# State-space stage: the second half's step size made by GpSimd inside the rounds, one convolution and the direct term on TensorE

## The reference, cut to what matters

```
x = einsum(in_proj_w, ctx)                       # per half: 256 channels x 512 positions
xc = depthwise causal conv(x, conv_w), 4 taps
u = silu(xc + conv_b)
dt_lo, Bm, Cm = split(x_proj_w @ u)              # 8, 16 and 16 rows
delta = softplus(dt_proj_w @ dt_lo + dt_proj_b)  # the step size
A = -exp(A_log)
for t: state = state * exp(delta_t * A) + (delta_t * u_t) * B_t ;  y_t = state . C_t
y = y + D * u
y = y * silu(z)                                  # z is the layer-normed x
```

## Time and profile before

| | us |
|---|---|
| median of 3 runs | 1015.46 (1014.79 to 1017.61) |
| the profiled execution, whole | 1015.46 |
| its span in the trace | 1012.7 |
| TensorE busy in the span | 911.6 (90%) |
| VectorE busy | 718.1 (71%) |
| ScalarE busy | 646.1 (64%) |
| GpSimd busy | 484.5 (48%) |

### The profile page before, as it was taken

One profiled execution on the slowest core, in us unless ns is written; L12 is line 12 of the kernel. 1 busy time (PEld: TensorE's weight loads), 2 busy tenths in 40 slices (PEclk: granted clock), 3 DMA queues, 4 the chain that ended last, 5 costly groups with the idle time before them and its releaser, 6 DMA issues.

```text
span 1012.7 us, 15673 instructions
## 1 busy us (share of the span) xinstructions
PE 911.6 (90%) x5322; PEld 747.7 (74%) x5322; DVE 718.1 (71%) x1301; ACT 646.1 (64%) x1252; POOL 484.5 (48%) x480
## 2 busy tenths in 40 slices
PE   5367677677999999999989999999999999999998
PEld 1022223346899999999977888888888888888887
DVE  7799998995777777777657675786665655666554
ACT  5857764685777777777665676656667644554553
POOL 0166653034676666666444343454344544344342
PEclk8589979797899999999999999999999999999999
DMA  9300100002100000000008611221112500021121
GB/s 289 157 0 1 62 2 0 1 1 99 60 1 1 2 1 2 1 2 1 2 33 305 216 54 52 58 65 56 43 53 63 230 1 2 1 74 53 60 65 44
DMA packets 17466, 55.97 MB, mean 55 GB/s; under 512 B 3057, under 2 KB 4185, under 8 KB 15245
## 3 DMA queue, kind: packets, MB, share of 16 engines
q1 hardware_dynamic: 5197, 34.01, 9.2%
q10 hardware_dynamic: 12192, 20.98, 6.9%
HBM read 53.82 MB, written 1.16 MB: 54 GB/s over the span
## 4 chain that ended last, share of the span: by engine, by line
PE 51%; DVE 12%; POOL 7%; issue 7%; ACT 4%; ACTq 1%; DMA 1%; DVEq 0%; POOLq 0%
PE psum L431 15%; PE psum L433 14%; PE psum L432 14%; POOL a_P L1963 3%; DVE a_max L1676 2%; POOL a_rk L1890 2%; POOL a_rq L1898 2%; DVE psum L1607 1%; PE psum L825 1%; DVE psum L1809 1%; PE psum L749 1%; PE psum L683 1%; PE psum L785 1%; DVE bn_st L1293 1%; ACT L1110 1%
## 5 line engine op out<-in xcount | busy, mean ns | idle before, releaser
L431 PE MATMUL psum<-x_norm_T_hi,f_wgu_hi 128*128 128x512 f32 x400 | 160.3, 401 | 3.0 <-DVE f_h_lo L1816 3.0
L433 PE MATMUL psum<-x_norm_T_hi,f_wgu_lo 128*128 128x512 f32 x400 | 157.5, 394 | 0.0
L432 PE MATMUL psum<-x_norm_T_lo,f_wgu_hi 128*128 128x512 f32 x400 | 156.8, 392 | 0.0
L431 PE MATMUL psum<-f_wd_hi,f_h_hi 128*128 128x256 f32 x400 | 121.8, 304 | 0.1
L1607 DVE TENSOR_TENSOR psum<-f_silu,psum 128x512 f32<-128x512 f32 x100 | 69.3, 693 | 69.6 <-PE psum L433 46.8
L433 PE MATMUL psum<-f_wd_hi,f_h_lo 128*128 128x256 f32 x400 | 112.9, 282 | 0.0
L432 PE MATMUL psum<-f_wd_lo,f_h_hi 128*128 128x256 f32 x400 | 112.9, 282 | 0.0
L1984 POOL TENSOR_TENSOR m_dBu<-m_du,m_Bs 128x1024 f32<-128x1024 f32 x32 | 76.3, 2384 | 68.5 <-DVE m_du L1405 24.8
L1816 DVE TENSOR_TENSOR f_h_lo<-psum,f_h_hi 128x512 fp32r<-128x512 f32 x100 | 68.9, 689 | 51.7 <-ACT f_h_hi L871 51.1
L1903 POOL TENSOR_TENSOR f_wgu_lo<-f_w,f_wgu_hi 128x512 fp32r<-128x512 f32 x44 | 56.8, 1292 | 93.9 <-ACT f_wgu_hi L871 93.9
L1903 POOL TENSOR_TENSOR f_wgu_lo<-f_wb,f_wgu_hi 128x512 fp32r<-128x512 f32 x36 | 46.6, 1295 | 103.2 <-ACT f_wgu_hi L871 103.2
(11 more groups left out here) (317 smaller groups left out, 2630.9 us busy)
## 6 DMA issues: line engine op xcount, KB each, us to landing
f_cw<-r_rows ACTq DMA_DIRECT2D x38, 256.0 KB, 3.2
f_wb<-in_f1b SPq DMA_DIRECT2D x6, 1152.0 KB, 8.9
f_w<-in_f3w SPq DMA_DIRECT2D x1, 5376.0 KB, 16.3
f_wa<-in_f1a SPq DMA_DIRECT2D x1, 3840.0 KB, 11.8
w_raw<-in_w0raw SPq DMA_DIRECT2D x1, 3072.0 KB, 18.9
...
```

What stands on the lines that cost most here:

```text
L431: mm(out, wh, xh, start=start, stop=False, **kw)
L432: mm(out, wh, xl, start=False, stop=False, **kw)
L433: return mm(out, wl, xh, start=False, stop=stop, **kw)
```

## The change

It makes these edits, all in the state-space stage:

- A new load `taps` (the convolution weights of channels 0 to 127, written out over 128 x 4 x 128, 256 KB) stands in the list between small and x. GpSimd multiplies it by the input projection (m_tap_w). TensorE then makes the convolved tile (h = 1, e = 0) straight from the context by four products shifted by one position each. VectorE's convolution of that tile goes, and ScalarE's silu of it reads PSUM.
- Relu(v) moves from ScalarE to VectorE (`positive_part`), and so does the bf16 copy of the 96 rows.
- D * u moves to TensorE: GpSimd makes two diagonal matrices (m_diag_D), and `direct(h)` starts each half's sum in PSUM with two products. The L1434 instructions go, and `gated(h)` multiplies PSUM by the gate.
- `delta(0)` is done in two pieces of 512 columns, one for each e, and so are round 0's m_dBu and its waits.
- `delta(1)` leaves VectorE; GpSimd does its three instructions one by one after the m_dBu of rounds 3, 6 and 9. The inverse of half 1 is made by ScalarE after round 0's exps instead of before round 0, and goes to another tile (m_split).
- The three weight sums stand in rounds 1, 2 and 3, one in each, instead of in round 0.
- Second half: the layer-norm statistics of its rows come before the first gate scales, and their variance after.

The core of the diff:

```diff
@@ TensorE, start
-            for h in range(2):
-                for e in range(2):
-                    mm(ps[:, 4 * h + e, :], m_in[...], ctxT[...], start=True, stop=True).then_inc(S("m_x"), 1)
+            for h, e in ((0, 0), (0, 1), (1, 1)):
+                mm(ps[:, 4 * h + e, :], m_in[...], ctxT[...], start=True, stop=True).then_inc(S("m_x"), 1)
+            pe.wait_ge(S("m_prepared"), 1)
+            for s_ in range(4):
+                last = mm(dst[:, :, s_:DM], tapw[:, 3 - s_, :], src[:, :, 0:DM - s_], start=s_ == 0, stop=s_ == 3, ...)
+            last.then_inc(S("m_x"), 1)
@@ TensorE, rounds
+            def direct(h):
+                pe.wait_ge(S("m_prepared"), 2)
+                for e in range(2):
+                    mm(ps[:, e, :], diagD[:, e, :], u[h][:, e, :], start=True, stop=False)
...
+            direct(0)
...
                     if g == NS + 1:
-                        pe.wait_ge(S("m_y_read"), 1)
+                        pe.wait_ge(S("m_yz"), 1)
+                        direct(1)
@@ ScalarE
-                copy(bcs[h][:, :], ps[0:96, 2 + 4 * h, :]).then_inc(S("m_p1"), 1)
...
-                    last = A(dlt[h][:, e, :], ps[:, 4 * h + e, :], ACT.Relu, bias=b_)
...
                 if g == 0:
-                    for i in range(3):
-                        last = link(sum_weights(i)) if i < 2 else sum_weights(i)
-                    last.then_inc(S("wabs_part"), 1)
+                    inverse(1)
+                if g in (1, 2):
+                    link(sum_weights(g - 1))
+                if g == 3:
+                    sum_weights(2).then_inc(S("wabs_part"), 1)
@@ VectorE
+                link(V.tensor_copy(bcs[h][:, :], ps[0:96, 2 + 4 * h, :]))
...
+            def positive_part(h):
+                dve.wait_ge(S("m_abs"), 2 * h + 2)
+                for e in range(2):
+                    last = V.tensor_scalar(dlt[h][:, e, :], ps[:, 4 * h + e, :], small[...], 0.0, ALU.add, ALU.max)
+                last.then_inc(S("m_xs"), 1)
...
-            conv(1, 0)
+            row_stats(1, 0, TH)
             gate_scales(0)
-            stats(1)
+            variance()
             conv(1, 1)
...
-                    last = V.scalar_tensor_tensor(dlt[h][:, e, :], u[h][:, e, :], small[...], ps[:, e, :], ALU.mult, ALU.add)
@@ GpSimd
+        loaded(pool, "m_in", "taps")
+        G.tensor_tensor(tapw[:, :, :], tapw[:, :, :], bc(m_in[:, 0:P].unsqueeze(1), [P, 4, P]), ALU.mult).then_inc(S("m_prepared"), 1)
...
+                    if g in (3, 6, 9):
+                        delta1(g // 3 - 1)
```

97 lines of the change are left out of this document (63 added, 34 removed).

## The result

| | before | after |
|---|---|---|
| median | 1015.61 us (1014.79 to 1017.61, 4 runs) | 1006.02 us (1005.51 to 1007.99, 4 runs) |
| the profiled execution, whole | 1015.46 | 1007.99 |
| its span | 1012.7 | 1006.2 |

The ratio is 0.9908 [0.9895, 0.9921], and the medians differ by 9.6 us, where 6.2 had been forecast. The direction was right, the size a third short, and the time lies just under the range's lower end. The profiled execution is the slowest of its four; the spans of the other three are 1003.7, 1003.8 and 1004.6. So the miss has to be looked for in three places: in the stage, in what differs from one execution to the next, and around the span.

A forecast was written before the change was run, and what follows sets the result against it. VectorE was taken as the bound, busy 47.5 of 48.6 us in steady rounds. Lead at round 4, change of halves, its price and the end: 4.7 + 1.4 - 0.1 + 0.2 = 6.2; 1015.46 - 6.2 = 1009.3 us, range 1006.3 to 1013.2.

The forecast's parts named there:

- The load and x_dbl: Start: taps delay m_dtw by 1.0, x_dbl starts at 14.4; ScalarE decides, silu of (1, 1) about 2.5 earlier.
- Exp to the scans: VectorE, half 0's exp to first scans: 12.2 of old list plus 0.7, 1.5, 0.5 and a stop; lead 6.0.
- The stop of L1431: Half 0's delta, e = 1: VectorE locked out by GpSimd's half product, 1.25 us, bounds 0 and 2.5.
- The first rounds: Rounds 1 to 4: GpSimd's product and the weight sums take 0.65 each, leaving a lead of 4.7 at round 4.
- GpSimd's steps: Half 1's delta after rounds 3, 6 and 9: next product 1.17 late, idle time absorbs it; cost 0.
- the tap products: TensorE at the start: eight records take 3.5 us, ending at 13.3 inside the wait for m_dtw.
- a TensorE that stays slow in the rounds: Rival, early rounds: low clock lasting six rounds longer loses 9.6 us, giving 1018.9; chance 0.06.
- the one of the tap products: Rival, start: shifted products sit on the path at low clock, 3.5 lost, put at 1013.3; chance 0.13.
- More is won: Rival: no stop (1.25), rounds 1 to 4 lose no more than before (1.3); 1006.8, chance 0.12.
- one more stop with three overruns of 1.0 in place of 0.6: Rival, first rounds: extra 1.25 stop and full weight-sum overruns, about 2.6 more, 1011.9; chance 0.13.
- Change of halves: Round 16: removing L1434 gains 1.40; TensorE's two added products cost 0.1, bound 1.8 at low clock.
- Around the span: Outside the profiled span: 2.8 us carried over unchanged from the kernel before, no gain counted.

The follow-up runs named there:

- after_again: The changed kernel run once more with nothing edited, for a second profile; 1006.61 us, ratio 0.9911.
- conv_on_vector: The changed kernel with the convolution of tile (1,0) back on VectorE, without tap weights or shifted products, statistics in their old order; 1009.77 us, ratio 0.9944.
- direct_only: The changed kernel with both the convolution and half 1's delta back on VectorE; ratio 1.0001 to the kernel before.
- late_copy: The changed kernel with ScalarE's copy of B for round g + 2 behind both exps of round g instead of between them; 1004.60 us, ratio 0.9890.
- smooth_ramp: late_copy with the third weight sum in round 4 and round 1's m_dBu on GpSimd in two halves; 1003.93 us, ratio 0.9902.
- longer_tensore: The kernel before with four small extra products on TensorE ahead of the first broadcast of B; 1013.91 us, ratio 0.9993.

## Why the prediction was right or wrong

Two steps failed in what they took for the cause: the taps' load that was to push x_dbl to 14.4, and with it the claim that ScalarE decides the start; and the 2.8 us around the span, carried over as unchanged without a reason. Two more terms had the right cause and the wrong size: VectorE from the exp to half 0's last m_du, and the first rounds.

**The load and x_dbl: the mechanism was wrong.** The forecast took the 261 GB/s of 5 to 10 us for a limit, so that 256 KB more cost 1.0. With the taps in the list the same window brought 319 GB/s (319 to 362 in the nine profiles with the taps, 261 to 306 in the eight without), and x_dbl started at 13.38 (12.57 in after_again), not at 14.4. ScalarE was then ready for the silu of (1, 1) at 19.70, 3.2 earlier than before and not 2.5, and waited 0.28 for VectorE's convolution. So the silu came 3.13 earlier (19.98 against 23.11), about as the removed 3.05 says. By an estimate from these rows, an x_dbl at 14.4 would have made ScalarE ready at 20.7, near the forecast's 20.6: its order of the two engines hung on this load. x did not come later either: it landed 6.3 to 8.6 us after its issue with the taps and 7.6 to 9.8 without. conv_on_vector shows VectorE's part by its first scan, 3.1 later. This step is 0.6 of the miss.

**Exp to the scans.** 15.5 us from the exp to the end of m_du(e = 1) instead of 16.15. The stop of L1431 is 0.95 and not 1.25: it began 0.48 after GpSimd's product and lasted about as long as that product still ran (38.92 to 40.01), not for a whole one. The other 0.4 is VectorE's list: the two positive parts take 1.3 and not 1.5, and the instructions of the old list 12.0 and not 12.2, mostly at L1424. 0.7 of the miss. That the wait for the inverse falls away was right, but with nothing to spare: it was there at 36.11, and VectorE's L1430 began at 36.14.

The Trainium skill's rule ("SBUF — State Buffer", "Who interferes with whom") is a lock of the two engines for a whole instruction where the VectorE instruction has two SBUF inputs and GpSimd's reads SBUF. The trace agrees: 0.95 on 0.69, and 2.03 on 1.22 in direct_only's L1431 (3.25), while the scans beside a GpSimd that is busy 36.3 of 48.2 us keep their 2.34.

**The first rounds.** 0.7 lost between round 0 and round 4, not 1.3. GpSimd's product of round 1 cost 0.54 (a wait of 1.09 where 0.55 was), near the 0.65 forecast; of the sums only the 0.26 in round 4 shows, where 0.65 had been counted. 0.6 of the miss. late_copy and smooth_ramp show that the 1.09 hides what ScalarE owes.

**GpSimd's steps, direct(0), the tap products.** Right: the rounds behind g = 3, 6 and 9 are 3.54, direct(0) stands at 38.35 to 41.43 in TensorE's waiting, and eight records took 3.65 (3.5 forecast). The rival of a TensorE that stays slow in the rounds, and the one of the tap products, didn't come.

**The range and the rivals.** *More is won* has the nearest time, 1006.8, by causes that did not come: the stop was there, and the first rounds lost 0.7 more than before. Two sums of the forecast do not follow from their own terms. Half the stop (0.6) and all of the first rounds' 1.3 reach down to 1007.4 and not to 1006.3, so that by them the measured time would lie further out. And one more stop with three overruns of 1.0 in place of 0.6 is 3.65, or 1013.0, and not 2.6.

**Change of halves.** 1.4 won at `gated(0)`: right (6.57 to 8.0). The price of 0.1 for the two products has to be a distribution: 2.25 in one execution, 0.55 in another, and before has such a stall too, 1.76 at 142.88. I read one execution's second half as if it were fixed. At the end nothing was gained beyond the lead, as forecast within 0.2.

**Around the span.** Put at nothing; it fell from 2.8 (median over 72 runs of before 2.6) to 1.8. 0.8 to 1.0 of the miss. longer_tensore shows the same fall with nothing of the change but a longer program on TensorE.

The sum: 6.2 + 1.9 (0.6 + 0.7 + 0.6) is 8.1 of lead; after_again shows 8.3 at the stage's end. That they agree so closely is luck: 0.55 is lost in round 19, and 0.9 regained against the 1.76 that before happened to have in its one profile. With 0.8 to 1.0 around the span it is 8.9 to 9.1; the medians differ by 9.3 and 9.6. The remaining 0.2 to 0.7 is within what before's own runs scatter (1013.1 to 1017.1).
